# GCN and GGN edge sums by (tile, node block) visits with block sums held in PSUM, and a preparation without their own visit tables

## The reference, cut to what matters

```python
dst = jnp.minimum((6250 * jax.random.uniform(k, (100000,)) ** 2.0).astype(jnp.int32), 49999)
_o = jnp.argsort(dst, stable=True); src = src[_o]; dst = dst[_o]

# L1 (GCN): self loops with weight 1 are appended to row, col, w
deg = jax.ops.segment_sum(w, col, num_segments=n)
dis = jnp.where(deg > 0, jax.lax.rsqrt(deg), 0.0)
norm = dis[row] * w * dis[col]
xw = x @ W
out = jax.ops.segment_sum(xw[row] * norm[:, None], col, num_segments=n) + b

# L3 (GGN)
h = x @ W_in.T + b_in
m = h @ W_msg
agg = jax.ops.segment_sum(m[src], dst, num_segments=n_nodes)
gi = agg @ W_ih.T + b_ih; gh = h @ W_hh.T + b_hh      # then a GRU cell

x = _layernorm(x + L0_gat(...)); x = _layernorm(x + L1_gcn(...))
x = _layernorm(x + L2_relational(...)); x = _layernorm(x + L3_ggn(...))
```

## Time and profile before

| | |
|---|---|
| median of 3 runs | 6013.23 us (6009.44, 6013.23, 6026.37) |
| the profiled execution | 6018.44 us; its span 6016.5 us |
| mean granted TensorE clock | 0.694 |
| busy: PE, PEld, DVE, ACT, POOL | 61%, 51%, 60%, 25%, 69% |
| preparation, first phase | 0 to 90.2 us |
| preparation, second phase | 90.2 to 212.4 |
| `gcn_edges`, first gather to last addition | 2297.2 to 3293.8 |
| `ggn_edges`, first gather to last addition | 4920.5 to 5912.6 |

### The profile page before, as it was taken

The page is one execution under the profiler, slowest core; times in us unless marked ns, Lnnn a source line. Parts: engine busy times, 40 slices in busy tenths (PEclk is TensorE's granted clock), DMA queues, the critical chain, the costliest instruction groups (busy, mean ns, idle before and its releaser), DMA issues. The chain is left out here.

```text
span 6016.5 us, 106908 instructions
## 1 busy us (share of the span) xinstructions
PE 3699.8 (61%) x29332; PEld 3070.5 (51%) x29332; DVE 3610.2 (60%) x10962; ACT 1531.2 (25%) x3918; POOL 4144.0 (69%) x4416
## 2 busy tenths in 40 slices
PE   4765355566364344445555799999975864444556
PEld 2555355455353333445554577777754753344444
DVE  4699475699573235444554788888869952223235
ACT  0476000377100011000000455555540140000004
POOL 6677777377777746777776577777773447777772
PEclk8655698655596555555555899999987985555557
DMA  5687576488585544566772466666663732221221
GB/s 164 179 242 229 159 247 214 132 242 241 160 247 173 151 122 139 165 175 183 189 197 55 142 207 206 206 207 207 207 148 113 205 85 53 53 53 51 53 53 37
DMA packets 564739, 946.34 MB, mean 157 GB/s; under 512 B 122022, under 2 KB 225983, under 8 KB 563599
## 3 DMA queue, kind: packets, MB, share of 16 engines
q0 software_dynamic: 140576, 316.92, 21.1%
q1 hardware_dynamic: 263907, 405.95, 21.0%
q10 hardware_dynamic: 159712, 216.63, 11.7%
HBM read 705.34 MB, written 235.74 MB: 156 GB/s over the span
## 5 line engine op out<-in xcount | busy, mean ns | idle before, releaser
L256 POOL DMA_INDIRECT s_rows<-rel_tab,src_v x832 | 809.6, 973 | 272.5 <-issue 246.7
L256 POOL DMA_INDIRECT stash<-gat_tab,src_g x784 | 780.6, 996 | 251.8 <-issue 238.0
L256 POOL DMA_INDIRECT gcn_rows<-gcn_tab,src_g x784 | 751.9, 959 | 247.9 <-issue 236.2
L256 POOL DMA_INDIRECT ggn_rows<-ggn_tab,src_g x784 | 747.7, 954 | 248.3 <-issue 248.0
L256 POOL DMA_INDIRECT stash<-in_x,src_g x736 | 738.9, 1004 | 236.9 <-issue 223.1
L1595 PE MATMUL e_psb<-tmp,e_oh 128*128 x3328 | 553.4, 328 | 554.9 <-DVE e_oh L1566 459.3
L1595 PEld LDWEIGHTS e_psb<-tmp,e_oh 128*128 128x128 f32 x3328 | 495.7, 231 | 612.9 <-issue 612.8
L2108 PE MATMUL gcn_pso<-gcn_rows,gcn_oh 128*128 x1952 | 500.9, 438 | 484.1 <-SPq L965 396.4
L1940 PE MATMUL ggn_pso<-ggn_rows,ggn_oh 128*128 x1952 | 470.0, 417 | 492.2 <-SPq L965 486.1
L2108 PEld LDWEIGHTS gcn_pso<-gcn_rows,gcn_oh 128*128 128x128 f32 x1952 | 431.2, 325 | 510.2 <-issue 510.2
L1940 PEld LDWEIGHTS ggn_pso<-ggn_rows,ggn_oh 128*128 128x128 f32 x1952 | 405.8, 308 | 557.0 <-issue 557.0
(11 more groups left out here) (502 smaller groups left out, 8071.9 us busy)
## 6 DMA issues: line engine op xcount, KB each, us to landing
edge_v<-stash SPq DMA_DIRECT2D x392, 256.0 KB, 2.2
g_lo_rows<-lo_rows ACTq DMA_DIRECT2D x392, 256.0 KB
e_values<-edge_v SPq DMA_DIRECT2D x392, 256.0 KB, 4.2
oh_dram<-tmp ACTq DMA_DIRECT2D x208, 256.0 KB
s_oh<-oh_dram SPq DMA_DIRECT2D x208, 256.0 KB
edge_v<-acc SPq DMA_DIRECT2D x208, 256.0 KB
r_values<-edge_v SPq DMA_DIRECT2D x208, 256.0 KB, 3.0
tmp<-drel_rows ACTq DMA_DIRECT2D x208, 128.0 KB
```

The source lines that it names most:

```text
L256: pool.indirect_dma_start(rows[:, t, :], None, tab[:, :], bass.IndirectOffsetOnAxis(ap=edges[:, t:t + 1], axis=0)).then_inc(s_land, 16)
```

## The change

**The two stages.** Both now go by tiles. POOL (`ring_gathers`) has 16 buffers (WSLOTS) of four rows of tiles and, from group 16 on, waits until `4 x (g - 3)` visits are done. `announce` is gone. PE (`ring_sums`) first sets the first banks to `acc` by a matmul with the identity; then come the 208 iterations of four visits. A visit's matmul adds to the bank of its block and increments the semaphore. Iteration n waits for group n (as long as n < 196), for the preset of the newest block among its visits, and for its one-hots. ScalarE (`evict`) waits for a block's last visit, copies its bank to `acc`, and presets the bank for the block `count` further on. GGN has eight banks, and PE loads its registers for two iterations at once (block of the last visit, banks, buffers). GCN has four banks (FEW) and loads for each iteration: blocks of the four visits, block of the last one, banks, buffers. VectorE adds no more to `acc`. One-hots are made up to four iterations ahead (RING), in GCN by four TENSOR_SCALARs per iteration as before, from `drel_v` and `tm_v`, in GGN by one TENSOR_TENSOR of 128x512.

**The time mask in GCN.** SP now issues the digit loads and the stores; VectorE copies the node times out of PSUM; the chain that makes the mask stands behind the last iteration and is kept in a part of `tmp` until the last one-hots have read the edge weights out of `tm_v`.

**The preparation.** The own tables, `edge_rows`, the fetch at L408 and all that leads to it are gone. `grow` is loaded straight from the inputs by nine DMAs. Half of the weight loads move from ScalarE's queue to SP's, ahead of the stores of the kept groups. POOL gathers its 12 groups in one go.

```diff
-        def gather_rows(pool, rows, tab, s_row, s_used):
+        def ring_gathers(pool, rows, tab, s_row, s_o):
             for g in range(GROUPS):
-                k = g % SLOTS
-                if g >= SLOTS:
-                    n = pool.value_load(done_row[0:1, g - SLOTS:g - SLOTS + 1], min_val=1, max_val=V)
-                    pool.wait_ge(s_used, n + RING)
+                if g >= WSLOTS:
+                    pool.wait_ge(s_o, GT * (g - 3))
...
-        def announce(sp, s_row, s_landed):
-            for g in range(GROUPS):
-                sp.wait_ge(s_row[g % SLOTS], (g // SLOTS + 1) * (16 * GT))
-                sp.sem_inc(s_landed, 1)
+        def evict(act, ps_b, count, b, s_o, s_tk, s_ev):
+            n = act.value_load(ends_row[0:1, b:b + 1], min_val=1, max_val=VT)
+            act.wait_ge(s_o, n)
+            nc.scalar.activation(acc[:, b * D:(b + 1) * D], ps_b[:, b % count, 0:D], ACT.Copy).then_inc(s_tk, 1)
+            if b + count < BLOCKS:
+                act.wait_ge(s_tk, b + 1)
+                preset(act, ps_b, count, b + count, s_ev)
+        def ring_sums(pe, ps_b, count, bank_of, oh, rows, s_row, s_oh, s_ev, s_o, beside=None):
+            its = count // GT
+            for b in range(count):
+                nc.tensor.matmul(ps_b[:, b, 0:D], ident[:, :], acc[:, b * D:(b + 1) * D], start=True, stop=True).then_inc(s_ev, 1)
+            for n in range(ITERS):
+                if n % its == 0:
...
+                    newest = pe.value_load(blkv_row[0:1, here.stop - 1:here.stop], min_val=0, max_val=BLOCKS - 1)
+                    banks = several(mybir.EngineType.PE, bank_of[0:1, here], count - 1)
+                    slots = several(mybir.EngineType.PE, wslot_row[0:1, here], WSLOTS * GT - 1)
+                    pe.wait_ge(s_ev, newest + 1)
+                if n < GROUPS:
+                    pe.wait_ge(s_row[n % WSLOTS], (n // WSLOTS + 1) * (16 * GT))
+                pe.wait_ge(s_oh, n + 1)
+                for t in range(GT):
...
+                                     start=False, stop=True, skip_group_check=True).then_inc(s_o, 1)
+                if beside is not None:
+                    beside(n, blocks)
@@ ggn_edges, VectorE
-                                i = v_.tensor_scalar(oh[:, k % 2, t, :], iota[:, :], dst_tab[:, col_], None, ALU.is_equal)
...
-                            v_.tensor_tensor(ab, ab, ps_o[k % 2][:, 0:D], ALU.add).then_inc(s_acc, 1)
+                        for n in range(ITERS):
+                            if n >= RING:
+                                dve.wait_ge(s_o, (n + 1 - RING) * GT)
+                            v.tensor_tensor(oh[:, n % RING, :, :], iota[:, :].unsqueeze(1).to_broadcast([P, GT, P]),
+                                            drel_v[:, n * GT:(n + 1) * GT].unsqueeze(2).to_broadcast([P, GT, P]), ALU.is_equal).then_inc(s_oh, 1)
@@ gcn_edges, VectorE
+                        for n in range(ITERS):
+                            onehots(n)
...
+                            static(n)
+                            if n >= 2:
+                                times(n - 2)
+                        times(ITERS - 2)
+                        times(ITERS - 1)
@@ preparation, POOL
-                    for g in range(EARLY):
-                        gather_early(g)
-                    pool.wait_ge(s_gv, 1)
-                    for c in range(VC):
-                        pool.indirect_dma_start(er[:, c, :, :].rearrange("p a e -> p (a e)"), None, edge_rows[:, :],
-                                                bass.IndirectOffsetOnAxis(ap=gvi[:, c:c + 1], axis=0)).then_inc(s_er, 16)
-                    for g in range(EARLY, KEPT_FIRST):
+                    for g in range(KEPT_FIRST):
                         gather_early(g)
@@ preparation, SP
+                    weights(sp, later)
                     for g in range(KEEP):
                         kept(g)
```

458 lines of the change are left out of this document (140 added, 318 removed).

## The result

The changed kernel takes 6178.62 us, median of 4 runs (6175.18 to 6183.29), against 6014.9 for the kernel before (4 runs): ratio 1.027, interval 1.0252 to 1.0288. That is 164 us more; 106 more were forecast, and the time lies 19 us above the upper end of the range. The profiled execution took 6183.29 us, its span 6181.5.

What follows compares the result with a forecast made beforehand. POOL's indirect gathers were taken to bound the kernel, 69% of the span. Preparation -11, GGN tail +19, GCN tail +43 and GGN one-hots +55 summed to +106 us: 6124 on the profiled execution, 6119 at the median, range 6050 to 6160.

Steps and rivals of the forecast that it cites:

- Preparation: First phase: POOL's 15.0 us wait and 2.5 us fetch go, a new wait of 6.5 comes; gain 11 us, between 3 and 17.
- the blocked issues on SP's list: Preparation: some 15 us of blocked issues ahead of SP's first store of a kept group, which leaves at 37 to 48.
- One-hots: GGN: the one-hot TENSOR_TENSOR delays every fourth gather by 0.30 us, over 185 groups +55 us, between 37 and 75.
- The lock: GGN: PE follows the landing, VectorE follows PE, so each one-hot keeps leading the next fourth gather by 0.25 us.
- the relation that I had read: GGN, from the trace: a gather loses about 0.55 us less the VectorE operation's lead, nothing when the gather leads.
- GCN tail: GCN end: 13 iterations left after the last landing, 12 at 3.0 us, then the mask chain in the open; +43 us.
- The mask chain: GCN end: the mask's VectorE operations, table load and tanh, hidden before, now about 7.3 us in the open.
- GGN tail: GGN end: 13 iterations left after the last landing, 20.9 us plus 0.3 for the eviction, less 2.6 before; +19 us.
- Inside the stages: GCN and GGN between first and last gather: the saved matmuls and additions ran under the gathers; no gain, 0 us.
- The stretches that were left alone: Second phase with GAT layers, and the relational block: nothing changed there, 0 us.
- That no gather is delayed: Rival, GGN: one-hots come after the gather's start or don't stop gathers; 6064 us (6045 to 6080), chance 0.22.
- The worse phase: Rival, GGN: one-hot lead under 0.1 us, loss 85 to 100 us instead of 55; 6149 to 6170, chance 0.07.

Runs made afterwards that it cites:

- prep_indices_first: Changed kernel with indices of all 12 kept groups loaded ahead of `grow`: first phase ends at 105.67 us; 7959.77 us where the kernel before took 7955.23.
- prep_through_dram: Changed kernel with `grow` copied to DRAM first, then loaded by one DMA: first phase ends at 92.47 us; 7898.54 us, kernel before 7955.23 on that chip.
- prep_indices_first_weights_back: Changed kernel with all 12 groups' indices first and all weight loads on ScalarE's queue: first phase ends at 101.17 us; 7923.14 us, kernel before 7955.23.
- ggn_four_scalars: Changed kernel with GGN one-hots made by four TENSOR_SCALARs per iteration again: 6116.5 us, ratio 1.017 to the kernel before.
- groups_by_register: Changed kernel with four TENSOR_SCALARs in GGN and PE waiting for the group its newest visit needs, announced by SP: 6099.51 us, ratio 1.0142.
- prep_dram_indices_first_weights_back: Changed kernel with `grow` through DRAM, all 12 groups' indices first, all weight loads on ScalarE's queue: first phase ends at 81.57 us; 6151.23 us.
- mask_ahead_repeated: Changed kernel with four TENSOR_SCALARs in GGN and GCN's time mask done two iterations at a time in the first 24, run again: 6089.14 us, ratio 1.0133.

## Why the prediction was wrong

The direction stands, and so do the mechanisms of the one-hots and of the tails. The preparation came out with the wrong sign, two further terms were too small, so nearly all errors went to the same side. With the -11 of the sum in place of the +17.8 the time would have been 6150, inside the range.

- **Preparation, -11 forecast, +17.8 measured.** This is the step that failed. I charged the removed wait as a gain and then looked for what is next only at the store of the first kept group, which I had leaving at 37 to 48 us; it left at 73.5. The term that was mis-sized is the blocked issues on SP's list: I took some 15 us, from the earlier trace rows; there were 50.2 us (23.0, 15.2 and 12.0). I also missed a wait: the seven index loads stand behind the loads of `grow`, and before, the 15 us of waiting for the table covered them. That alone cost little, since with the indices first POOL waits as long for the store (`prep_indices_first`, 2 us). `prep_through_dram` shows that the loads straight into SBUF are the part that the change brought in, 15.5 us; the weight loads cost 4.5 us, in `prep_indices_first_weights_back`. What blocks SP there was not settled. The DMA queues of the changed kernel between 10 and 50 us (packets, MB, share of the 16 engines; q1 is SP's, q10 ScalarE's, q0 POOL's) show only that it is not the engines' bandwidth: they are busy for 30% of the time, and SP's queue moves least.

```profile
q10 hardware_dynamic: 1695, 2.00, 14.5%
q0 software_dynamic: 580, 1.19, 11.2%
q1 hardware_dynamic: 291, 0.55, 3.8%
```

- **One-hots, +55 forecast, +75.0 measured.** The lock is as predicted: PE starts 1.74 us behind the end of its fourth gather (5501.25 to 5502.99 in the timeline above, 1.79 in the earlier trace rows) and VectorE 2.10 behind PE; the three runs with other one-hots or another phase bear it out. The one-hots themselves cost 68 us (1060.4 less the 992.8 of `ggn_four_scalars`), inside the 37 to 75 that were stated. The size was off: the lead is 0.17 us, not 0.25, and the delay 0.39 instead of 0.30. By the relation that I had read, 0.55 less the lead, the 0.17 give 0.38. A difference of 0.08 us in a sum of two durations is some 15 us of the time. The other 7 us are mostly a MEMSET (below), which was not in the sum.
- **GCN tail, +43 forecast, +49.1 measured.** 12 steps of 3.56 us, not 3.0, are 6.7 us more; I saw VectorE's addition go, and did not charge PE's own loads and issues for the mask, 1.3 us of the 3.56. From the last gather to PE's start it took 5.9 us, 4.3 before; the profiles with the same GCN code have 4.5 to 7.6. The mask chain went the other way: from 3355.68 to 3361.52 it took 5.8 us, not 7.3, and the table load that I had counted from the earlier trace rows does not stand in it.
- **GGN tail, +19 forecast, +18.4 measured**, and `groups_by_register` takes 14.3 of it back. Right; its 13 iterations took 22.0 us, and 20.9 were worked out.
- **Inside the stages, 0 forecast.** GGN is right, once the one-hots are out: 992.8 us, with 6.4 of it at the MEMSET. GCN grew by 5.5 us, all of it longer gathers: those that began beside the bf16 TENSOR_SCALARs of the mask (L1911 and L1912) lost 6.6 us, 2.4 before, and those beside the one-hots 3.8, 1.9 before. Whether the operations caused it was not tried.
- **The stretches that were left alone, 0 forecast.** The -5.2 and +4.4 of the table are not clear of what profiles of the same code differ by: the second phase with the GAT layers lies between 2196.4 and 2207.0 us in all profiles from chips like these, the relational block between 1615.3 and 1632.4.
- **The rivals.** That no gather is delayed, for which the Trainium skill, SBUF — State Buffer, section "Who interferes with whom", would speak with its tensor_tensor that stalls no DMA from POOL (the section calls the reason inferred, and says beside it that with both inputs in SBUF such an operation contends with GpSimd's reads), is refuted: 71 us. The worse phase, 85 to 100 us for a lead under 0.1, has the nearest time (6149 to 6170), and by its mechanism it is wrong: the lead was 0.17.

The range was too narrow, since the preparation could not come out as a loss in it.

## What to carry to other kernels

A wait that is removed is a gain only up to the next thing that it covered: list for the waiting engine every input that it will now ask for earlier, and for each the place in its queue. Where two engines run in step, a few tenths of a microsecond in their phase can be worth more than the work saved: here 0.39 us of shift (0.17 ahead to 0.22 behind) were 65 us of a stage of 1060. Shift one of them and measure before thinking about the work itself. A static wait that must hold for all inputs (group n in iteration n) turns into a tail: count the iterations that stand behind the last landing, and charge each at the rate of its engine's own stream.

## What was not expected of the hardware

- A gather beside a MEMSET on VectorE took as long as the MEMSET, or longer, or nothing more at all. In the changed kernel the first GGN gather took 7.78 us beside one of 5.61 that began 0.71 us behind it; before, the gather began 0.34 us ahead of the MEMSET, took 1.03, and the next ones, inside it, 0.95 and less. It is not the phase alone: beside the MEMSET of `x_n` in the preparation a gather that began 0.23 us ahead took 0.94 before, and 6.7 us in `prep_dram_indices_first_weights_back`. One gather was held at both MEMSETs, for 6.7 to 9.2 us, in all 13 profiles of the changed kernel and its edits, and none in the three of the kernel before and its edits. What decides was not tried.

```profile
4920.51 1.03 POOL L256 DMA_INDIRECT ggn_rows<-ggn_tab,src_g  x1 [9.79 <-issue]
4920.85 5.61 DVE L1869 MEMSET acc<- 128x6664 f32 x1 [5.57 <-issue]
4921.85 0.95 POOL L256 DMA_INDIRECT ggn_rows<-ggn_tab,src_g  x1 [0.30 <-issue]
...
4992.09 7.78 POOL L247 DMA_INDIRECT ggn_rows<-ggn_tab,src_g  x1 [9.13 <-SPq L1749]
4992.80 5.61 DVE L1757 MEMSET acc<- 128x6664 f32 x1 [5.50 <-issue]
```

- What stands ahead of a DMA in its queue changes its cost. Nine direct loads (three each to 98, 97 and one partition) took SP 45.4 us to issue, nine copies from DRAM to DRAM 6. With seven more loads of four-byte pieces ahead of the copies the wait for these ended at 41.0 us instead of 24.2, in the kernel before, where nothing else on SP's list up to there was changed.
- PE's iteration with four visits and no mask takes 2.28 us in the tail of `mask_ahead_repeated` (2.23 to 2.39), whether its eight matmul passes are busy for 1.15 us at the high clock or for 2.07 at the low: its stream of register loads and issues is the bound there.
